# Delta rule: merging the 32-blocks with 32x32 products, and a projection ahead of the 64x64 level

## The reference

```python
def short_conv(x, w):            # causal, 4 taps, then silu
    ...
q = l2norm(short_conv(hidden_states @ Wq, conv_wq)); k = l2norm(short_conv(hidden_states @ Wk, conv_wk))
def step(S, inp):                # per head, token after token
    qt, kt, vt, gt, bt = inp
    S = S * jnp.exp(gt)
    delta = (vt - kt @ S) * bt
    S = S + kt[:, None] * delta[None, :]
    return (S, qt @ S)
```

## Time and profile before

| | us |
|---|---|
| median of 3 runs | 2114.64 (2112.45 to 2114.76) |
| profiled execution | 2113.24 |
| its span | 2111.6 |
| PE busy, share of the span | 1671.7, 79% |
| DVE, ACT, POOL busy | 1039.3, 659.0, 683.6 |
| delta rule on PE, first projection to the last solve's stage | 930.5 to about 1755 |
| one projection copy on ACT (L1548), mean | 0.687 |
| one tap on DVE (L1717), mean | 0.746 |

### The profile page before, as it was taken

One profiled execution on the slowest core, in us unless ns is written; L12 is line 12 of the kernel. 1 busy time (PEld: TensorE's weight loads), 2 busy tenths in 40 slices (PEclk: granted clock), 3 DMA queues, 4 the chain that ended last, 5 costly groups with the idle time before them and its releaser, 6 DMA issues. The chain is left out here.

```text
span 2111.6 us, 28929 instructions
## 1 busy us (share of the span) xinstructions
PE 1671.7 (79%) x10666; PEld 1071.2 (51%) x10666; DVE 1039.3 (49%) x2374; ACT 659.0 (31%) x1167; POOL 683.6 (32%) x1092
## 2 busy tenths in 40 slices
PE   4797887887948886858799999999999962777771
PEld 3343444444425554423566666666666752545651
DVE  3745445454213333555367666666766421334623
ACT  3151331522311211545244454444445210111010
POOL 2020200200000000015767777777777711000152
PEclk8999798999968888989899999999999765898596
DMA  1000000000020001430121222222122113110173
GB/s 45 1 2 1 20 1 1 21 1 11 1 71 20 20 20 36 132 65 15 36 51 28 43 41 41 51 51 49 28 46 33 28 26 99 55 65 30 33 165 105
DMA packets 216824, 83.93 MB, mean 40 GB/s; under 512 B 166249, under 2 KB 211666, under 8 KB 216706
## 3 DMA queue, kind: packets, MB, share of 16 engines
q1 hardware_dynamic: 205266, 67.90, 14.5%
q0 software_dynamic: 5376, 12.59, 2.4%
q10 hardware_dynamic: 6064, 1.86, 0.4%
HBM read 50.60 MB, written 31.72 MB: 39 GB/s over the span
## 5 line engine op out<-in xcount | busy, mean ns | idle before, releaser
L1717 DVE SCALAR_TENSOR_TENSOR d_conv<-d_prep,k_cw,d_conv 128x511 f32<-128x511 f32 (+2 forms) x288 | 214.2, 746 | 32.7 <-ACT d_conv L1548 26.0
L1669 POOL TENSOR_TENSOR d_prod<-d_blk 64x30 f32<-64x30 f32 (+4 forms) x360 | 173.6, 482 | 102.0 <-DMA d_blk<-mid_a_blk 74.8
L1334 PE MATMUL d_prep<-k_hT,k_w 128*128 128x512 f32 x384 | 187.9, 614 | 21.6 <-POOL d_power L1643 12.4
L1673 POOL TENSOR_TENSOR d_blk<-d_blk,d_prod 64x30 f32<-64x30 f32 (+4 forms) x360 | 184.3, 512 | 28.2
L419 ACT ACTIVATE a_probs<-a_acc 128x896 f32<-128x896 f32 x128 | 117.4, 917 | 219.6 <-PE a_acc L244 131.8
L516 DVE TENSOR_REDUCE a_top<-a_turn 128x4 f32<-128x512 f32 (+3 forms) x240 | 147.3, 652 | 62.4 <-PE a_turn L207 54.3
L465 POOL TENSOR_TENSOR a_rstd<-a_rstd,a_mhalf 128x4 f32<-128x4 f32 x4 | 4.1, 1027 | 407.9 <-DVE a_rstd L565 407.9
L1334 PEld LDWEIGHTS d_prep<-k_hT,k_w 128*128 128x128 f32 x384 | 68.0, 197 | 82.1 <-issue 48.1
L1373 PE MATMUL d_prep<-d_kq 128*128 128x256 f32 x384 | 95.5, 393 | 15.1 <-DVE d_qkT L1749 15.1
L1548 ACT ACTIVATE d_conv<-d_prep,k_cw 128x512 f32<-128x512 f32 x96 | 65.9, 687 | 130.4 <-PE d_prep L1334 130.1
L1373 PEld LDWEIGHTS d_prep<-d_kq 128*128 128x128 f32 x384 | 73.4, 198 | 44.4 <-DVE d_qkT L1749 26.9
(11 more groups left out here) (352 smaller groups left out, 3687.7 us busy)
## 6 DMA issues: line engine op xcount, KB each, us to landing
mid_gate<-p_gate SPq DMA_DIRECT2D x4, 768.0 KB, 3.4
mid_v<-p_v_tok SPq DMA_DIRECT2D x4, 768.0 KB, 3.5
d_v_h<-mid_v SPq DMA_DIRECT2D x12, 256.0 KB, 5.6
d_gate_h<-mid_gate SPq DMA_DIRECT2D x12, 256.0 KB, 5.5
mid_a_blk<-d_AT SPq DMA_DIRECT2D x48, 64.0 KB, 2.0
d_blk<-mid_a_blk SPq DMA_DIRECT2D x12, 256.0 KB, 3.5
mid_u_blk<-d_blk SPq DMA_DIRECT2D x12, 256.0 KB, 2.9
mid_l_blk<-d_blkT SPq DMA_DIRECT2D x12, 256.0 KB, 3.7
```

The source lines that it names most:

```text
L1334: last = nc.tensor.matmul(PB[f % 2][:], w[:, n % 2, i, k, :], hT[:, k, b * T:(b + 1) * T], start=k == 0, stop=k == CK - 1)
L1669: nc.gpsimd.tensor_tensor(pr, blk[:, 0:t, t:t + 1].broadcast_to([lanes, t, m]), blk[:, t:t + 1, t + 1:BLK].broadcast_to([lanes, t, m]), AL ...
L1673: nc.gpsimd.tensor_tensor(blk[:, 0:t, t + 1:BLK], blk[:, 0:t, t + 1:BLK], pr, ALU.subtract).then_inc(subst, 1)
L1717: ins = nc.vector.scalar_tensor_tensor(dst, PB[f % 2][:, 0:T - j], cw[:, n % 2, f % 2, TAPS - 1 - j:TAPS - j], dst, ALU.mult, ALU.add)
```

## The change

- The second level is made of 32x32 products (`PAIRS` names the two pairs of 32-blocks in a tile). X takes 8 matmuls a batch in place of 4; L takes 16 in place of 4, because each pair makes L21 and, by a second product with the operands swapped, its transpose U12. The transposes (`level2_u`) and their copies go.
- `U32` and `L32` go. The gather writes the diagonal blocks straight to U and L, and waits for the third-level products and the last solve of the head before.
- The new blocks are copied into L and U by four copies a batch, on ACT for the first and third batch of `ORDER`, on DVE for the second and fourth (semaphores `lu_act`, `lu_dve`). `level3` waits for these.
- The X products of the first two batches stand ahead of the last batch's `differences` and `correlate`, those of the other two behind them.
- The first projection of the next head (`project(q + 1, 0)`), with its copy on ACT and its taps on DVE, moves from the start of `recur` to the end of `turn`: on PE ahead of `level3`, on ACT ahead of the X3 cuts, on DVE behind the copies.

```diff
@@ gather_blocks (SP)
                 if n:
-                    sp.wait_ge(l2_e, BATCH * n)
+                    sp.wait_ge(x3, BATCH * n)
+                    sp.wait_ge(solved, CH * n)
                 for j in range(NB):
                     r = slice(BLK * j, BLK * (j + 1))
-                    sp.dma_start(U32[r, :, r], u_blk[j, :, :, :].rearrange("c s t -> s c t")).then_inc(inv_back, 16)
-                    sp.dma_start(L32[r, :, r], l_blk[j, :, :, :].rearrange("c s t -> s c t")).then_inc(inv_back, 16)
+                    sp.dma_start(U[r, :, r], u_blk[j, :, :, :].rearrange("c s t -> s c t")).then_inc(inv_back, 16)
+                    sp.dma_start(L[r, :, r], l_blk[j, :, :, :].rearrange("c s t -> s c t")).then_inc(inv_back, 16)
@@ PE
+        PAIRS = [(slice(64 * k, 64 * k + BLK), slice(64 * k + BLK, 64 * k + 2 * BLK)) for k in range(2)]
...
                 pe.wait_ge(k_ready, BATCH * n + i + 1)
-                times(ORDER[i], AT[:, n % 2, :, :], L32).then_inc(x2, 1)
+                b = ORDER[i]
+                for c in range(CH):
+                    for r, q in PAIRS:
+                        last = nc.tensor.matmul(LB[b][q, c, r], AT[r, n % 2, b * CH + c, q], L[r, b * CH + c, r], start=True, stop=True)
+                last.then_inc(x2, 1)
 
             def level2_l(n, i):
                 pe.wait_ge(x2_e, BATCH * n + i + 1)
-                times(ORDER[i], U32, X2).then_inc(l2, 1)
-
-            def level2_u(n):
-                for i, b in enumerate(ORDER):
-                    pe.wait_ge(l2_e, BATCH * n + i + 1)
-                    for c in range(CH):
-                        last = nc.tensor.transpose(LB[b][:, c, :], L[:, b * CH + c, :], ident[:])
-                    last.then_inc(u2, 1)
+                b = ORDER[i]
+                for c in range(CH):
+                    for r, q in PAIRS:
+                        nc.tensor.matmul(LB[b][q, c, r], U[q, b * CH + c, q], X2[q, b * CH + c, r], start=True, stop=True)
+                        last = nc.tensor.matmul(LB[b][r, c, q], X2[q, b * CH + c, r], U[q, b * CH + c, q], start=True, stop=True)
+                last.then_inc(l2, 1)
...
                 for i, b in enumerate(ORDER):
-                    pe.wait_ge(u2_e, BATCH * n + i + 1)
+                    pe.wait_ge(lu_act if i % 2 == 0 else lu_dve, BATCH // 2 * n + i // 2 + 1)
@@ turn (PE)
-                    for b in range(1, BATCH):
+                    for b in range(1, BATCH - 1):
                         differences(q, b)
                         correlate(q, 2 * b)
                         correlate(q, 2 * b + 1)
                 if 0 <= m < D_H:
-                    for i in range(BATCH):
-                        level2_x(m, i)
+                    level2_x(m, 0)
+                    level2_x(m, 1)
+                if q < D_H:
+                    differences(q, BATCH - 1)
+                    correlate(q, 2 * BATCH - 2)
+                    correlate(q, 2 * BATCH - 1)
+                if 0 <= m < D_H:
+                    level2_x(m, 2)
+                    level2_x(m, 3)
                     for i in range(BATCH):
                         level2_l(m, i)
-                    level2_u(m)
+                    if q + 1 < D_H:
+                        project(q + 1, 0)
                     level3(m)
@@ recur (PE)
-                    if ahead:
+                    if ahead and c:
                         project(n + 2, 2 * c)
@@ turn (ACT)
-                    for i, b in enumerate(ORDER):
-                        act.wait_ge(u2, BATCH * m + i + 1)
-                        nc.scalar.activation(U[:, rows[b], :], LB[b][:], ACT.Copy).then_inc(u2_e, 1)
+                    for i in (0, 2):
+                        b = ORDER[i]
+                        act.wait_ge(l2, BATCH * m + i + 1)
+                        for r, q in PAIRS:
+                            cut(L[:, rows[b], :], LB[b], q, r)
+                        for r, q in PAIRS:
+                            cut(U[:, rows[b], :], LB[b], r, q, lu_act if r.start else None)
+                    if ahead < D_H:
+                        begin(ahead)
+                        convolve(ahead, 0)
@@ keep_l, turn (DVE)
-                nc.vector.tensor_tensor(L[:, rows[b], :], LB[b][:], L32[:, rows[b], :], ALU.add).then_inc(l2_e, 1)
+                for r, q in PAIRS:
+                    nc.vector.tensor_copy(L[q, rows[b], r], LB[b][q, :, r])
+                for r, q in PAIRS:
+                    ins = nc.vector.tensor_copy(U[r, rows[b], q], LB[b][r, :, q])
+                ins.then_inc(lu_dve, 1)
...
-                    for i in range(BATCH):
-                        keep_l(m, i)
+                    keep_l(m, 1)
+                    keep_l(m, 3)
+                    if q + 1 < D_H:
+                        convolve(q + 1, 0)
```

More of the change, by code:

```diff
@@ L1218, in layer1_delta_rule @@
         prod = sb("prod", [NB * TILES, BLK * BLK // 4])
-        U32, L32 = sb("U32", [P, TILES, P]), sb("L32", [P, TILES, P])
         U, L = sb("U", [P, TILES, P]), sb("L", [P, TILES, P])
@@ L1239, in layer1_delta_rule @@
          gu_ready, diff, decayed, kk, attn, blk_out, blk_in, subst, inverted, inv_out, inv_back, k_turned, k_ready, x2, x2_e,
-         l2, l2_e, u2, u2_e, x3, x3_e, u3, u3_e, from_k, from_q, r_ready, fs_ready, solved, eps_ready, added, s_ready, s_dec,
+         l2, x3, x3_e, u3, u3_e, from_k, from_q, r_ready, fs_ready, solved, eps_ready, added, s_ready, s_dec,
          o_ready, mean_ready, rms_ready, o_done, stored, cchain, nchain, rchain) = (sem(n) for n in (
@@ L1243, in layer1_delta_rule @@
             "n_ready", "pow_ready", "gu_ready", "diff", "decayed", "kk", "attn", "blk_out", "blk_in", "subst", "inverted",
-            "inv_out", "inv_back", "k_turned", "k_ready", "x2", "x2_e", "l2", "l2_e", "u2", "u2_e", "x3", "x3_e", "u3", "u3_e",
+            "inv_out", "inv_back", "k_turned", "k_ready", "x2", "x2_e", "l2", "x3", "x3_e", "u3", "u3_e",
             "from_k", "from_q", "r_ready", "fs_ready", "solved", "eps_ready", "added", "s_ready", "s_dec", "o_ready",
@@ L1248, in layer1_delta_rule @@
         oqT_ready, fqT_ready, oq_turned, fq_turned = sem("oqT_ready"), sem("fqT_ready"), sem("oq_turned"), sem("fq_turned")
+        lu_act, lu_dve = sem("lu_act"), sem("lu_dve")
         w_in, v_in = [sem(f"w_in{n}") for n in range(2)], [sem(f"v_in{n}") for n in range(3)]
@@ L1375, in correlate @@
                 last.then_inc(kk, 1)
-            def times(b, left, right):
-                for c in range(CH):
-                    last = nc.tensor.matmul(LB[b][:, c, :], left[:, b * CH + c, :], right[:, b * CH + c, :], start=True, stop=True)
-                return last
             def turn_out(n, c):
@@ L1572, in recur @@
                 ahead = n + 2 < D_H
-                if ahead:
-                    begin(n + 2)
                 for c in range(CH):
@@ L1579, in recur @@
                     if ahead:
-                        convolve(n + 2, 2 * c)
+                        if c:
+                            convolve(n + 2, 2 * c)
                         convolve(n + 2, 2 * c + 1)
@@ L1616, in turn @@
                         decay_up(q, b)
+                ahead = q + 1
                 if 0 <= m < D_H:
@@ L1639, in _ @@
         def _(pool):
-            for m, value in ((U32, 0.0), (L32, 0.0), (X2, 0.0), (ones, 1.0), (mhalf, -0.5)):
+            for m, value in ((U, 0.0), (L, 0.0), (X2, 0.0), (ones, 1.0), (mhalf, -0.5)):
                 nc.gpsimd.memset(m[:], value).then_inc(consts, 1)
```

## The result

The changed kernel took **2130.39 us** (median of 4 runs, 2127.18 to 2134.61) against 2114.7: ratio 1.0077, interval 1.0065 to 1.0089. It is 0.8% slower where 0.4% faster was forecast, outside the range, and the sign is wrong.

What follows compares the result with a forecast made beforehand. PE's own work bound the kernel before; after the change the blocks' round trip, 60.9 us a head, would. Start +2.4, nine intervals -8.1 and last turn -2.9 make -8.6: 2106.0 us against the median, range 2094 to 2122.

Steps and rivals of the forecast that it cites:

- The cost of a 32x32 pass: PE's X and L products: 30 ns a pass, half the 64x64 price, with bounds of about 16 and 59 ns.
- the lower bound worked out from the earlier trace: 32x32 passes on PE: two quadrant pairs side by side could halve 30 ns to about 16.
- PE's own loop: PE's work for one head: saves 2.3 to 2.4 us, 59.4 instead of 61.8.
- rival 3: X and L products: small passes cost 59 ns like 64x64 ones, PE's loop 65.0 us, total 2154; 7%.
- The round trip as the bound: Middle heads: blocks' trip from spread through POOL to next spread takes 60.9 us and binds; a head gains 0.9.
- First head: First turn: forming now stands behind the wait for the blocks, so the spread of head 1 comes at 1036.4, before 1028.20.
- Last turn: Last turn, from landing of the blocks to the solve: 11.9 us instead of 14.8, 2.9 less.
- the sum: Whole kernel: 2.4 - 8.1 - 2.9 = -8.6 us for start, nine intervals and last turn.
- rival 2: PE's wait before its first X batch drops the clock, 1.6 us a time, nine times 14.4: 2120.4; 20%.
- The moved projection: Ahead of the 64x64 level: covers DVE's last copy, 1.4 us otherwise; its convolution taps on DVE worth nothing either way.
- the ten intervals: Middle heads, from the spread of head 1 to the last spread: -13.9 us forecast.

Runs made afterwards that it cites:

- the version with small products only: Changed kernel with all X batches behind the last forming and the projection back at the start of recur: 2116.36 us, ratio 1.0006.
- the longer trips: Extra POOL work in each block inversion: changed kernel 2147.88 us, with all X behind the forming 2111.3; kernel before 2117.12, with two X batches ahead 2136.91.
- X behind: Changed kernel with all four X batches again behind the last batch's differences and correlations, the rest as changed: 2091.7 us, ratio 0.9877.

## Why the prediction was wrong

**The cost of a 32x32 pass: taken at 30 ns, measured 15 to 16.** X of two batches stands at 0.69 us for 32 passes, and 64 passes took 1.20 in the version with small products only. Less the end of the last pass (about 0.2), that is 16 ns from start to start, the lower bound worked out from the earlier trace rows, not half of the 64x64 price. So correlations to solve fell to 8.4 us, 6.5 us less than before; 0.6 of it is the two X batches that now stand ahead (0.69 in the row, its last pass's end included), so PE's own loop is about 5.9 us shorter where 2.4 was forecast. By this term alone the result should have been better than forecast.

The Trainium skill (TensorE: Matmul & The Clock Gate, Back-to-back issue gap), which has about 62 ns for each matmul where hardware decode is off, would have made rival 3. The trace does not agree: 15 to 16 ns for a pass, about 31 for an fp32 matmul of two. Rival 3 is out.

**The round trip as the bound: right, and 0.7 us too short.** The waits of 0.7 to 3.7 us before the first X products are there in eight of ten heads, and the longer trips show the loop. Its parts are 54.4 us in the mean (spread to last gather issue, 53.1 in the earlier trace rows), 2.4 for the landing, 4.7 from there to the spread in the least disturbed heads: 61.6, not 60.9. The way from the landing to the spread is 0.6 shorter than forecast, by the cheap passes; the trip to the last gather issue is 1.3 longer, and 0.8 of this is the four spread issues of SP, 2.8 us in the mean against 2.0 (with full products they are at 1.9 in nearly all heads). What lengthens them was not settled. 61.6 against 61.8 before means that the middle heads gain nothing. That is one failure, worth 7 us: the trip was to let 0.9 of PE's saving through, and at 61.6 it lets 0.2.

**First head: right.** First spread at 1036.4 forecast, 1038.66 found, in an execution whose delta rule starts 3.2 later. **Last turn: right in its place, lost behind it.** Landing to solve takes 11.8 us (before 14.8, forecast 11.9). That it meets the forecast is luck: the passes are half as dear as assumed, but the whole stretch ran at half clock (0.50), where 1.6 us had been set aside for it. The clock stays at 0.50 until the end of the stage, where it was 0.64 before, and 1.2 of 3 us are left.

**The step that failed: the sum has nothing for the clock in the middle heads.** It was left to rival 2, priced at 14 us and given 20%, because a stretch in which PE stood still for 1.4 us had kept its clock. Ten intervals at 61.6 would be 616 us; they took 631.7. By the rows, the 16 us left over lie in two places:

- 7.5 us between the X products and the spread, in the four heads that waited 2.1 to 3.7 us for the blocks, 1.6 us in three of them and 2.6 in the fourth. This is rival 2 as it was written, at its price, in four heads of ten. In the run with idle products ahead of the wait it is gone: all ten heads take 4.75.
- 8.4 us between the landing and the X products, because PE came late; 6.5 of it is the one interval behind the slow stretch from 1288 to 1306. The fall there began in the 32x32 products with the pause of 1.29 us, not at a wait for the blocks. The waits of PE for DVE in the forming, 22.1 us in ten heads against 13.7 before, can have a part in the rest; this was not tested.

Without the 16 the change would stand at 2114, no change.

**The moved projection was put at "worth nothing", and that failed too.** Back at its old place it gives 12 us (2118.2 against 2130.4), and moved alone in the kernel before it costs 13. Without it, PE goes from the 64x64 level to the solve with narrow products and a pause of 0.47 us only, and the next product runs at half clock (1365.19). With small products and X behind the same move gains 24.7 us. So its sign depends on what stands around it, and no run explains all three. The version with small products only never waits for the blocks and has a fall in every head, so the wait for the blocks is not the only cause. What the falls shown away from that wait (1288, 1350, 1365) have in common is a stretch of 32x32, 64x64 or 128x32 products with a pause of 0.47 to 1.29 us in it; whether the narrow products or the pauses do it stays open.

The Trainium skill (TensorE: Matmul & The Clock Gate, What's actually happening) says that the gate follows how busy PE has been. The trace agrees in part: PE stood still 2.1 to 3.7 us ahead of four falls, and was busy 2.86 of 4 us ahead of the one at 1350. But it was busy 4.53 of 5 us ahead of the fall at 1365, and a stretch of 2.63 of 4 us kept its clock, so busy time alone does not sort these.

**In sum:** of -13.9 us forecast for the ten intervals, +9.3 came: 7 us of the difference from the trip that is 0.7 longer, 7.5 from slow forming behind the waits, 8.4 from PE's late arrival, most of it behind one long fall. With X behind, PE's saving shows in part, 59.96 instead of 62.2 us from spread to spread, though its clock falls as well.

## What to carry to other kernels

Before work is put ahead of a producer to fill a wait, close the loop: if the work waits for something that this same producer started one iteration earlier, the round trip becomes a lower bound of the iteration, and everything saved elsewhere is lost. An engine that gets faster also stands still for longer where another one now binds, and TensorE's clock can fall behind that wait: put a price on it. Count neither smaller products nor a move of a wide one as free; here the same move cost 13 us in one kernel and gained 25 in another, so read the granted clock by head and try it. Undoing each piece alone is cheap and found 39 us here.

## What was new about the hardware

- Fp32 passes of 32x32 (two for a matmul) follow each other at 15 to 16 ns at the full clock, against about 59 for the 64x64 ones of the earlier trace rows.
- The clock fell to half at four of eight waits of PE for the blocks (2.1 to 3.7 us), not at those of 0.7 to 2.2 us. It also fell where PE was busy 4.53 of 5 us with narrow products and one pause of 0.47 us. One fall cost about 1.6 us of forming; the longest one shown kept the stretch from 1288 to 1306 at 0.53. An idle 128x512 product of 1 us per head made a kernel some 6 us faster.
- In the dense stream of 32x32 passes PE stands still for 0.5 to 1.7 us in some heads of most versions with small products, with no releaser in the profile ("issue"). What this is stays open.
